# The last product of a feed-forward block, by Strassen's seven block products, with operands streamed from DRAM and a new order of the first work

## The reference

```python
mod = (_silu(c) @ wmod).reshape(4, 6, 1, -1)                # six rows of 1024 for each of 4 batches
sa, ca, ga, sb, cb, gb = (mod[:, i] for i in range(6))
ga = (2 * (ga >= 0) - 1) * jnp.maximum(jnp.abs(ga), 0.25)   # gb in the same way
h = _layernorm(x) * (1 + ca) + sa
x = x + ga * (h @ masked(attn_weight).T)                    # 1024 x 1024, masked by 32 x 32 blocks
h = _layernorm(x) * (1 + cb) + sb
h = silu(h @ w1.T) * (h @ w2.T)                             # 1024 -> 2752, weights decoded from 4-bit codes
x = x + gb * (h @ w3.T)                                     # 2752 -> 1024
```

## Time and profile before

| | us |
|---|---|
| median of 3 runs | 1741.81 (1741.48 to 1742.3) |
| the profiled execution, its own time | 1741.88 |
| its span, first to last instruction | 1740.2 |
| TensorE busy in the span | 1672.0 |
| ScalarE busy | 868.5 |
| VectorE busy | 525.7 |

### The profile page before, as it was taken

How to read it: one execution, slowest core, us unless ns; L and a number is a source line. 1 busy time by engine, 2 the same in 40 slices (tenths; PEclk the granted TensorE clock), 3 DMA queues, 4 the chain that set the end, 5 groups by cost and what they waited for, 6 DMA issues and landing times.

```text
span 1740.2 us, 18667 instructions
## 1 busy us (share of the span) xinstructions
PE 1672.0 (96%) x7684; PEld 1363.7 (78%) x7684; DVE 525.7 (30%) x798; ACT 868.5 (50%) x1081; POOL 9.1 (1%) x11
## 2 busy tenths in 40 slices
PE   3879999999999999999999999999999899999997
PEld 1657788888888888888888888888788688787886
DVE  3577786521111111111111111111333311311212
ACT  2445576986666666666666666664422111111110
POOL 1000000000000000000000000000000000000000
PEclk8889999999999999999999999999999899999999
DMA  9774322342222222222222222231454412412413
GB/s 373 276 259 163 130 97 98 96 134 92 88 88 88 88 89 88 88 88 88 88 88 88 88 88 88 88 99 49 140 145 140 147 49 85 122 49 82 125 48 130
DMA packets 73694, 197.28 MB, mean 113 GB/s; under 512 B 7746, under 2 KB 13250, under 8 KB 73610
## 3 DMA queue, kind: packets, MB, share of 16 engines
q1 hardware_dynamic: 73610, 196.10, 34.3%
HBM read 141.25 MB, written 54.82 MB: 113 GB/s over the span
## 4 chain that ended last, share of the span: by engine, by line
PE 88%; DMA 4%; DVE 4%; ACT 3%; issue 1%; SPq 0%; DVEq 0%; ACTq 0%
PE ps L1398 26%; PE ps L1347 18%; PE ps L1349 18%; PE ps L1348 18%; PE ps L1271 2%; PE ps L1273 2%; PE ps L1272 2%; PE ps L1233 2%; DMA w_raw<-w_d 2%; DMA weight_piece<-wT 1%; PE ps L1216 1%; ACT modulated L632 1%; DMA wmod<-wmod 1%; ACT decoded L597 0%; ACT early_decoded L610 0%
## 5 line engine op out<-in xcount | busy, mean ns | idle before, releaser
L1347 PE MATMUL ps<-ffn_in_hi,w_hi 128*128 128x512 f32 x1344 | 524.0, 390 | 0.0
L1349 PE MATMUL ps<-ffn_in_hi,w_lo 128*128 128x512 f32 x1344 | 523.2, 389 | 0.0
L1348 PE MATMUL ps<-ffn_in_lo,w_hi 128*128 128x512 f32 x1344 | 523.1, 389 | 0.0
L597 ACT ACTIVATE decoded<-decoded 128x1024 f32<-128x1024 f32 (+1 forms) x441 | 467.8, 1061 | 14.0
L1349 PEld LDWEIGHTS ps<-ffn_in_hi,w_lo 128*128 128x128 f32 x1344 | 252.3, 188 | 52.5
L1347 PEld LDWEIGHTS ps<-ffn_in_hi,w_hi 128*128 128x128 f32 x1344 | 252.4, 188 | 52.1 <-DVE h_tile L1073 0.3
L1348 PEld LDWEIGHTS ps<-ffn_in_lo,w_hi 128*128 128x128 f32 x1344 | 252.4, 188 | 52.1
L788 ACT ACTIVATE h_hi<-h_raw 128x512 fp32r<-128x512 f32 x88 | 55.6, 632 | 404.6 <-PE ps L1398 369.4
L1398 PE MATMUL ps<-w_hi,h_hi 128*128 128x512 f32 x704 | 221.7, 397 | 7.9 <-DVE w_hi L1130 5.9
L827 DVE SCALAR_TENSOR_TENSOR decoded<-decoded,w_scale 128x1024 f32<-128x1024 f32 (+1 forms) x63 | 77.2, 1226 | 502.7 <-ACT decoded L597 502.7
L1398 PE MATMUL ps<-w_hi,h_lo 128*128 128x512 f32 (+1 forms) x704 | 221.1, 395 | 0.0
(11 more groups left out here) (95 smaller groups left out, 967.1 us busy)
## 6 DMA issues: line engine op xcount, KB each, us to landing
wmod<-wmod SPq DMA_DIRECT2D x12, 2048.0 KB, 11.1
h_raw<-h_d SPq DMA_DIRECT2D x88, 256.0 KB, 3.1
h_d<-h_tile SPq DMA_DIRECT2D x84, 256.0 KB, 2.8
codes<-w12q SPq DMA_DIRECT2D x41, 512.0 KB, 3.6
w_raw<-w_d SPq DMA_DIRECT2D x22, 512.0 KB, 4.0
w_scale<-w3s SPq DMA_DIRECT2D x43, 256.0 KB, 5.0
codes<-w3q SPq DMA_DIRECT2D x21, 512.0 KB, 4.2
w_d<-decoded SPq DMA_DIRECT2D x21, 512.0 KB, 4.0
```

Of the source, the lines that this page charges most:

```text
L597: act.activation(ACC[npar][0:rows, :], src[0:rows, :], ACT.Prelu, bias=bias, scale=sign, alpha=slope).then_inc(line_ready, 1)
L1347: pe.matmul(acc, RH[ring][:, k, :], HH[:, b, k, :], start=(k == 0), stop=False)
L1348: pe.matmul(acc, RH[ring][:, k, :], HL[:, b, k, :], start=False, stop=False)
L1349: last = pe.matmul(acc, RL[ring][:, k, :], HH[:, b, k, :], start=False, stop=(k == C - 1))
```

## The change

**Down stage.** The product is cut in two along tokens (1024 each), hidden features (11 chunks each, `HC`; the 22nd chunk is now padded with zeros to 128 rows) and output features (512 each). Strassen's scheme makes it of seven block products. Each is (sum or difference of one or two blocks of h) x (sum or difference of one or two blocks of w3). The seven run one after the other, each for eight token tiles `m` of 128 (`JT`). A tile is 11 chunks x 3 passes = 33 matmuls of 128 x 512 into one bank; there are 56 tiles.

An operand of a tile (S) is 128 x 1408, one or two loads of 721 KB from `h_d`, which the up stage now stores by token tile, in pieces of 512 B. VectorE adds (`s_add`) where there are two blocks, ScalarE rounds (`s_high`), VectorE makes the low part (`s_low`). The operand of a product (T) is 11 chunks of 128 x 512, which are loaded again for each product from `w3_d` (two blocks: 524 KB; one block: 262 KB) into one of two buffers `t_raw`, and go through `t_add`, `t_high`, `t_low`. The load of chunk g waits for the low part of chunk g - 2. `UNITS` says which chunks of the next product's T are handled beside which tile. The results collect in SBUF: a product is copied out of PSUM by ScalarE or added by VectorE; for the 32 finished 128 x 512 pieces VectorE adds, multiplies by the gate and adds the residual (`finish`).

**Order around the half step of the up stage.** The decoding of the last chunk of w3 moves into the step before. T's first 11 chunks and two tiles of S are made beside the half step's blocks.

**Early work.** ScalarE does `copy_rows(1)` and `input1(0)` ahead of `weight_high(0)`, and `input1(1)` ahead of `weight_high(2)`; VectorE does `read_mod(1)` and the two `low_part1` earlier; TensorE does the second `sum_partitions` behind `attend_half(0, 0)`; `WARM` is 24 for 16.

The core of the diff (`load_s` and `load_t` are SyncE's, the first loop over `m` is ScalarE's, `t_units` and the second loop are VectorE's, `down_tile` is TensorE's):

```diff
+PRODUCTS = [("m6", ((2, 1), (1, 1)), -1, ((1, 1), (1, 2)), 1),
+            ("m2", ((2, 1), (2, 2)), 1, ((1, 1),), 0),
+            ("m4", ((2, 2),), 0, ((2, 1), (1, 1)), -1),
+            ("m1", ((1, 1), (2, 2)), 1, ((1, 1), (2, 2)), 1),
+            ("m3", ((1, 1),), 0, ((1, 2), (2, 2)), -1),
+            ("m7", ((1, 2), (2, 2)), -1, ((2, 1), (2, 2)), 1),
+            ("m5", ((1, 1), (1, 2)), 1, ((2, 2),), 0)]
+UNITS = [(0, 1), (2,), (3, 4), (5, 6), (7, 8), (9,), (10,), ()]
+            def load_s(m):
+                p = m % 2
+                if m >= 2:
+                    sp.wait_ge(s_lo, m - 1)
...
+            def load_t(g):
+                q, i, k = g % 2, g // HC, g % HC
+                if g >= 2:
+                    sp.wait_ge(t_lo, g - 1)
...
+            def s_high(m):
...
+                if m >= 2:
+                    act.wait_ge(m_done, m - 1)
+                act.activation(SH[p][:], SR[p][0][:], ACT.Copy).then_inc(s_hi, 1)
...
+            for m in range(MTILES):
+                i, j = m // JT, m % JT
+                if m + 1 < MTILES:
+                    s_high(m + 1)
+                if m >= 1:
+                    copy_product(m - 1)
+                if i + 1 < len(PRODUCTS):
+                    for k in UNITS[j]:
+                        t_high(i + 1, k)
...
+            def t_units(i, units):
+                for k in units:
+                    t_add(i, k)
+                    if k >= 1:
+                        t_low(i, k - 1)
...
+            for m in range(MTILES):
+                i, j = m // JT, m % JT
+                if m + 1 < MTILES:
+                    s_low(m + 1)
+                if m >= 1:
+                    use_product(m - 1)
+                if i + 1 < len(PRODUCTS):
+                    t_units(i + 1, UNITS[j])
+                    if j == JT - 1:
+                        t_low(i + 1, HC - 1)
+                if m + 2 < MTILES:
+                    s_add(m + 2)
...
+            def down_tile(m):
+                i, j, p = m // JT, m % JT, m % 2
+                pe.wait_ge(s_lo, m + 1)
+                if m == 0:
+                    pe.wait_ge(h_made, TPB * (CH + 1))
...
+                for k in range(HC):
+                    if j == 0:
+                        pe.wait_ge(t_lo, i * HC + k + 1)
+                    pe.matmul(acc, SH[p][:, k, :], TH[i % 2][k][:], start=(k == 0), stop=False)
+                    pe.matmul(acc, SH[p][:, k, :], TL[i % 2][k][:], start=False, stop=False)
+                    last = pe.matmul(acc, SL[p][:, k, :], TH[i % 2][k][:], start=False, stop=(k == HC - 1))
```

593 lines of the change are left out of this document (297 added, 296 removed).

## The result

| | before | after |
|---|---|---|
| median, us | 1742.05 (1741.48 to 1742.32, 4 runs) | 1777.07 (1775.12 to 1780.08, 4 runs) |
| ratio to before | | 1.0204, interval 1.0192 to 1.0216 |
| profiled execution, its own time | 1741.88 | 1777.36 |
| its span | 1740.2 | 1775.6 |

The change makes the kernel 35 us slower; 1760, in a range of 1736 to 1783, was forecast. The forecast span was 1759.1 and the measured one is 16.5 us longer. Where those 16.5 us are is the first question; whether the mechanisms are the ones that the prediction named is the second.

What follows compares the result with a forecast made beforehand. TensorE was taken to bound the kernel nearly throughout, through its matmul count and waits. Start 1278.7 + matmuls 418.9 + clock 5 + waits 48 + clock 3 + end 7.5 - early work 2 = 1759.1 span; forecast 1760, range 1736 to 1783.

Steps and rivals of the forecast that it cites:

- Matmuls removed: Down stage: 1848 matmuls for 2080, 418.9 us against 492.4, a gain of 73.5 us if TensorE never waits.
- The start: Ahead of the down stage: T's loads come one at a time, 5.1 us a chunk; TensorE idles 40.0 us, until 1278.7.
- The waits beside the tiles: Down stage tiles: VectorE's rounds with T's loads in them outlast a tile of 7.48 us; 48 us in sum.
- three waits each of 3 to 5 us: Sign in the changed profile: TensorE waits for `s_lo` this often and this long in m2, m4, m1, m3.
- The clock: Down stage: half clock costs 5 us after the start gap and 3 beside the tiles; most hides in the next wait.
- rival 3: Down stage: the clock falls in each long gap and is not covered, 12 us more, 1772; 8%.
- The end: After the last matmul: two pieces on VectorE, a store and waits take 7.5 us, against 9.1.
- Early work: First attention products: first starts about 10 us earlier, a 4.9 us wait follows; -2 us, bounds -3 and +3.
- The quick loads (1): Rival, T and S loads: all land in 3.2 us, S at full-queue rate; 1739. Faster 15%, no difference 10%.
- The DMA rate (2): Rival, down stage: S at 270 GB/s or less costs m2, m1, m7, m5 1 us a tile; 1784; 12%.
- Only the matmuls (4): Rival, down stage: T's loads overlap and no gap comes at the start; 1665; 3%.

Runs made afterwards that it cites:

- even rounds: Kernel with the down stage's start reordered (1727.27 us), T chunks spread 1, 2, 1, 2, 1, 2, 1, 1 a tile, T and S loaded earlier, `s_add` moved: 1688.71 us.
- the start-alone run: Changed kernel, each T chunk's low part taken right after its own addition, for the first product's T alone: 1767.46 us, ratio to before 1.015.
- the fillers: Changed kernel with useless matmuls on TensorE ahead of tiles whose start waits (165 ahead of the first, 4 to 22 ahead of 17 others): 1781.6 us, ratio 1.0224.
- the run alone: Kernel before the change with only the new order of the early work: 1743.2 us against 1741.85, ratio 1.0006.
- the last version: Kernel with even rounds, T chunks 2 to 4 asked for ahead of the first S tile, which is treated after chunk 5: 1684.47 us, ratio 0.9674.

## Why the prediction was right, and which of its terms were not

**Matmuls removed.** 1848, at 0.2267 us each, 418.9 us: the kernel with even rounds takes 423.6 for them, 2.1 of it a wait.

**The start.** Forecast 1278.7 with 40.0 us of idle TensorE, measured 1279.06 and 39.1. The parts differ and cancel, so that the sum agrees to 0.4 us is in part luck. From one addition to the next, six chunks took 4.5 to 5.0 us for 5.1. Two took 7.2 and 6.8: one beside the first S tile, one whose load stood in SyncE's queue behind a store of the half step (issued at 1266.44). The loads began at 1220.0 for 1218.8, and chunk 2 was added at 1232.7, where its landing was forecast for 1230.7. The mechanism, one load at a time, is shown by the start-alone run (9.6 us).

**The waits beside the tiles: this is the term that was mis-sized.** Forecast 48 us at full clock, plus 3 + 5 for half clock. Measured from the starts of the tiles, each stretch less 7.48 us a tile, so waits and half clock together:

| tiles | in | forecast | measured |
|---|---|---|---|
| 0 | clock after the start gap | 5 | 2.0 |
| 1 to 2 | m6, third tile | 3 | 6.0 |
| 11 to 14 | m2 | 8 | 9.2 |
| 19 to 22 | m4 | 7.5 | 10.7 |
| 23 to 26 | switch m4 to m1 | 3 | 8.0 |
| 27 to 30 | m1 | 12 | 13.0 |
| 35 to 38 | m3 | 7.5 | 8.6 |
| 39 to 44 | switch and m7 | 6 | 8.8 |
| 52 to 55 | m5 | 1 | 3.7 |
| | clock, uncovered | 3 | (in the above) |
| | sum | 56 | 70.0 |

The places are those forecast, all of them. The sign "three waits each of 3 to 5 us" did not come: in m2, m4, m1 and m3 there are two or three waits each, of 0.9 to 5.0 us, and only four of them reach 3 us, since slow tiles fill part of each round. The long rounds themselves were well sized in three products and short in one. From one `s_lo` to the next VectorE took 11.2 to 11.7 us in m2 (11.8 forecast), 12.0 to 12.7 in m1 (12.5) and 11.6 to 11.7 in m3 (11.5), but 12.1 to 12.7 in m4 (11.5). The larger part of the 13.9 us is elsewhere: the switch from m4 to m1 5 us more than forecast, the third tile of m6 3, m4 3, the switch to m7 and m7 3, m5 3, m2, m1 and m3 1 each. The start's clock was 3 less, and the 3 for uncovered clock are in these numbers.

Three things were left out of the rounds. First, a VectorE operation on 512 columns that waits for the one before it takes 0.79 us from start to start, and one that does not 0.61, where 0.69 was taken for both. The six operations that finish m5's two pieces (four waiting, two not) take 4.4 us for 4.1, so a round is 8.98 us (1751.14 to 1760.12) for 8.7, and without slack each of the last two tiles waits 1.2 us. Second, loads of 256 KB take 4.0 us in the median, as long as 512 KB. In the long rounds 3.7 was taken, and VectorE waited 3.5 to 3.9 us in m2, 3.7 to 4.4 in m1, 4.0 in m3 and 4.3 to 4.6 in m4. Third, at a switch the first two chunks of the next T stand behind a store, a residual load and two S blocks in SyncE's queue and VectorE waits 2.6 us for them. Chunk 10 before them stands behind the first S of two blocks: its second load goes out after 1475.4, it is there at 1483.0, and VectorE waits 3.1 us. How much of the switch that is was not measured by itself (with most of the second S blocks gone the whole kernel gains 8.4 us).

**The clock.** The forecast said that most of it hides in the next wait and took 8 us. The trace seems to say 24.4, and rival 3 seems to have come true; the fillers show that most of it hides, as the forecast's own step had it. The page "TensorE: Matmul & The Clock Gate" of the Trainium skill, section "HAM oscillation", describes such tiles that start cold after each wait, and counts what they lose in full. In this trace the cold tiles are there, ten of them at 9.1 to 10.6 us for 7.5, but filling the gaps gained nothing here: in the long rounds another engine sets the start of the next tile.

**The end.** 7.5 us forecast, 7.7 measured. **Early work.** -2 forecast, about +1 measured in the trace, no difference in the run alone; the clock fell in the wait, as the prediction had allowed.

**The sum.** Start and early work +2.4, waits and clock +13.9, end +0.2: 1759.1 + 16.5 = 1775.6.

**Rivals.** The quick loads (1) did not come: 512 KB took 3.9 us, not 3.2. The page "DMA: Bandwidth & Descriptors" of the Trainium skill, section "Anatomy of one DMA", gives 2.0 us + bytes/436e3 for DMAs on the GpSimd path, which as an estimate is 3.2 us for 524 KB. The loads here are issued by SyncE, so the formula is not for them, and the measured median is 0.7 above it. The DMA rate (2) as what decides is refuted by two runs: with a fifth fewer bytes 38.6 us of waits stay, and with even rounds more bytes a microsecond are moved and the waits go. (Its price was also mis-added: m2, m1, m7 and m5 have 32 tiles, so 1 us each is 32, not 24.) Only the matmuls (4), 1665, is 19.5 us below the last version, which reaches 1684.5 once the loads do overlap and still has 12.2 us idle ahead of the first tile: it was a statement on what the change is worth, not on what it did.

## What to carry to other kernels

Draw the loop buffer by buffer: with two buffers and "use g, then free g - 1" only one load is ever on its way, and moving the release by one step cost nothing here and gave 37 us. Then even out the side work so that the helper's rounds are as long as TensorE's tile (7.5 us in most rounds after it, 9.2 in the longest, with slack to cover it): a queue of waits that sums to 45 us was removed without taking away one instruction. And before you blame a low clock, look at which engine sets the start of the next tile: what a slow tile loses ahead of a wait is mostly taken out of that wait.

## What the runs showed of the hardware that was not expected

The DMA queues moved 420 GB/s in a slice of 1.4 us (436 in the changed kernel's own trace) with loads of 512 KB and of 704 KB on their way, where the kernel before had shown 153 GB/s at a share of 0.53. Loads of 256 and of 512 KB landed after nearly the same 4.0 and 3.9 us. The length of a single gap does not tell whether the clock has fallen: the tile at 1399.43 started at half clock after 2.30 us (its first matmul lasts 0.79 us), the one at 1527.20 did not after 2.68 (0.50 us), and in the trace before a gap of 2.0 us had left the clock up (1.00 granted from 1239 to 1262 us).
